# Zeros on TensorE, four-way scores, and copies moved between VectorE and ScalarE in a two-layer vision tower

## The reference

```python
h = _L0_tok_ref(x, W, b)                       # patches @ W.T + b: (64, 64, 64)
h = h + _L0_attn_ref(_layernorm(h), ...)       # attention in 64 windows of 64 tokens, 8 heads of 8
h = h + _L0_ffn_ref(_layernorm(h), ...)        # graph-attention router, top 2 of 4 experts
h = h + _L1_attn_ref(_layernorm(h), ...)       # one head of 64, batch norm, relu
h = h + _L1_ffn_ref(_layernorm(h), ...)        # top 2 of 8 experts

def _L0_attn_ref(x, w_qkv, b_qkv, w_proj, b_proj, rel_pos_bias):
    qkv = (x @ w_qkv + b_qkv).reshape(NWb, W, 3, NUM_HEADS, HEAD_DIM).transpose(2, 0, 3, 1, 4)
    q, k, v = (qkv[0], qkv[1], qkv[2])
    attn = jnp.einsum('nhqd,nhkd->nhqk', q, k) * HEAD_DIM ** (-0.5)
    attn = jax.nn.softmax(attn + bias[None], axis=-1)      # bias[h, q, k] = rel_pos_bias[h, k - q + 63]
    out = jnp.einsum('nhqk,nhkd->nhqd', attn, v).transpose(0, 2, 1, 3).reshape(NWb, W, D)
    return out @ w_proj + b_proj
```

## Time and profile before

| what | value |
|---|---|
| device time of three runs | 793.17, 797.44, 798.47 us; median 797.44 |
| profiled execution | 796.66 us, its span 794.8 us |
| mean granted TensorE clock | 0.744 of full speed |
| busy: TensorE, its weight loads | 538.0 us (68%), 309.7 us (39%) |
| busy: VectorE | 561.4 us (71%) |
| busy: ScalarE, GpSimd | 350.3 us (44%), 279.0 us (35%) |

### The profile page before, as it was taken

The page is one execution under the profiler, slowest core; times in us unless marked ns, Lnnn a source line. Parts: engine busy times, 40 slices in busy tenths (PEclk is TensorE's granted clock), DMA queues, the critical chain, the costliest instruction groups (busy, mean ns, idle before and its releaser), DMA issues. The chain is left out here.

```text
span 794.8 us, 12363 instructions
## 1 busy us (share of the span) xinstructions
PE 538.0 (68%) x4174; PEld 309.7 (39%) x4179; DVE 561.4 (71%) x1303; ACT 350.3 (44%) x833; POOL 279.0 (35%) x340
## 2 busy tenths in 40 slices
PE   5606968499899785366567277724368848788986
PEld 4503535266566462133233234311246524222322
DVE  6994997988987585789997489885523466467453
ACT  1115536247577432244343134387533434555453
POOL 6003111112122023777777578700211102144334
PEclk9998557659899695555565565658569967799898
DMA  6100000000000005111111111000000000000001
GB/s 191 38 0 1 1 1 1 1 1 2 1 2 2 3 0 72 23 39 27 35 38 24 21 23 38 8 2 0 0 1 1 1 0 1 1 0 2 14 13 27
DMA packets 28632, 13.04 MB, mean 16 GB/s; under 512 B 22080, under 2 KB 25761, under 8 KB 28322
## 3 DMA queue, kind: packets, MB, share of 16 engines
q1 hardware_dynamic: 23842, 10.82, 5.5%
q0 software_dynamic: 4736, 1.51, 2.2%
HBM read 10.77 MB, written 1.54 MB: 15 GB/s over the span
## 5 line engine op out<-in xcount | busy, mean ns | idle before, releaser
L1532 POOL DMA_INDIRECT edge_scratch<-src_rows_dram,slot_src_index x144 | 152.9, 1062 | 46.5 <-issue 43.4
L607 POOL TENSOR_TENSOR wa_kbd<-wa_qk,headmask 128x512 f32<-128x512 f32 x32 | 35.3, 1104 | 157.1 <-ACT wa_qk L717 157.1
L494 POOL TENSOR_TENSOR ln_xs<-xn,ln_stats 128x256 f32<-128x256 f32 x32 | 19.7, 622 | 160.6 <-DVE ln_stats L462 94.7
L736 ACT ACTIVATE wa_probs<-wa_scores,wa_max 128x64 f32<-128x64 f32 x256 | 64.4, 335 | 8.1 <-DVE wa_max L784 7.9
L2015 DVE SCALAR_TENSOR_TENSOR moe_weighted<-moe_y_ps,moe_b_cols,moe_G 128x512 f32<-128x512 f32 x32 | 24.0, 750 | 47.1 <-ACT moe_G L1988 44.2
L2074 POOL TENSOR_TENSOR moe_acc<-moe_acc,moe_weighted 128x512 f32<-128x512 f32 x28 | 37.7, 1348 | 49.7 <-DVE moe_weighted L2015 49.6
L1703 PE MATMUL moe_h_ps<-xT,moe_w 65*128 65x512 f32 x64 | 54.3, 996 | 0.0
L1695 PE MATMUL edge_acc<-edge_scratch 128*64 128x64 bf16 x672 | 22.3, 236 | 47.2 <-DVE edge_scratch L118 47.2
L1974 ACT ACTIVATE moe_hidden<-moe_h_ps,moe_b_cols 128x1024 f32<-128x1024 f32 x32 | 35.5, 1113 | 41.1 <-PE moe_h_ps L1906 41.1
L555 PE MATMUL ln_pT<-ident,ln_xs 128*64 128x128 f32 (+1 forms) x112 | 22.1, 341 | 45.3 <-POOL ln_xs L494 44.4
L647 PE MATMUL wa_s_ps<-wa_kbd,wa_qk 64*64 64x512 f32 x128 | 45.7, 799 | 4.3 <-issue 3.7
(11 more groups left out here) (404 smaller groups left out, 1369.1 us busy)
## 6 DMA issues: line engine op xcount, KB each, us to landing
edge_onehot_T<-slot_lo_dram SPq DMA_DIRECT2D x16, 288.0 KB, 3.2
edge_scratch<-src_rows_dram,slot_src_index POOLq DMA_INDIRECT x144, 2.5
edge_scratch<-in_L_ffn_edge_index SPq DMA_DIRECT2D x2, 1024.0 KB, 6.3
xrow<-in_x SPq DMA_DIRECT2D x4, 256.0 KB, 7.7
out_h<-h SPq DMA_DIRECT2D x4, 256.0 KB, 2.6
moe_w<-in_L_ffn_W SPq DMA_DIRECT2D x3, 256.0 KB
src_rows_dram<-src_rows SPq DMA_DIRECT2D x1, 320.0 KB
moe_w<-in_L_ffn_W SPq DMA_DIRECT2D x2, 128.0 KB
```

Of the source, the lines that this page charges most:

```text
L607: pool.tensor_tensor(kbd[b][:], bc_at(qk[b][:, 1, :], 1, NH), bc(k.headmask[:, 0, :], WIN), ALU.mult).then_inc(kbd_ready, 1)
L736: ins = act.activation(pr[b][:, h, :], sc[b][:, h, :], ACT.Exp, bias=mx[b][:, h:h + 1], scale=-1.0)
L1532: pool.indirect_dma_start(gs[b][:, j, :], None, srow_dram, bass.IndirectOffsetOnAxis(edges.src_index[:, x:x + 1], axis=0))\
```

## The change

- **tokenize.** The reordering of the pixels (`take`) and the storing of the tokens (`save`) move from VectorE to ScalarE. VectorE makes the 16 pulls in a row, right after the weights' copy. `pick`, `pick_small`, the selects and the cast go.
- **First normalize.** After its statistics VectorE makes three pulls. PREFIX_STEP and MOVE_STEP become 6 and 11.
- **Scores.** The masked keys hold four heads at a time: row group g of a window (dimensions 32 g to 32 g + 31) holds heads 4 g to 4 g + 3, masked by a new 128x4 mask that VectorE makes at the start. Each tile has four products of 32 rows by 256 columns; group g goes to bank g of one score tile, which is used for every tile (`biased >= c`).
- **Zeros.** Ahead of the wait for the exponentials, TensorE multiplies zeros three times, 128x128 by 512 columns in bf16, into the bank that the turned exponentials then overwrite.
- **Router.** The two casts of the edge parts move to ScalarE; VectorE's second and third step stand between `match`, `spread` and the new `spread_far`.
- **Combine.** The block goes. VectorE weighs and adds quarters 2 and 3 right after the gates, ahead of the adds of quarters 0 and 1.

```diff
-PREFIX_STEP, MOVE_STEP, RING, AHEAD = 7, 12, 6, 2
+PREFIX_STEP, MOVE_STEP, RING, AHEAD = 6, 11, 6, 2
...
         @block.scalar
         def _(act):
-            for c in range(n):
+            def take(c):
+
+                act.wait_ge(loaded[c], 16)
+                if c > 1:
+                    act.wait_ge(turned, c - 1)
+                act.activation(patch[c % 2][:].rearrange("s j (p q) -> s j p q", p=8),
+                               xrow[c][:].rearrange("s (p j q) -> s j p q", p=8, j=8), ACT.Copy).then_inc(cut, 1)
...
+            def save(c):
+
+                act.wait_ge(mapped, c + 1)
+                act.activation(h[:, 8 * c:8 * c + 8, :], ph[c % 2][:], ACT.Copy).then_inc(saved, 1)
+
             take(0)
...
             take(1)
             for c in range(n):
+                turned_out(c)
                 if c + 2 < n:
                     take(c + 2)
                 save(c)
...
+        @block.vector
+        def _(dve):
+            for b in range(2):
+                dve.memset(xT[b][D:D + 1, :], 1.0).then_inc(ones, 1)
+            dve.wait_ge(weight_turned, 1)
+            dve.tensor_copy(k.wtok[0:D, :], weight_ps[:]).then_inc(weight_ready, 1)
+            for _ in range(16):
+                next(lists, None)
...
-            dve.tensor_copy(k.pick[:].rearrange("r p t (x m) -> r (p t x) m", x=2),
-                            bc(k.pick_small[:].rearrange("r p t x -> r (p t x)"), D))
...
+            if beside and not N:
+                for c in range(3):
+                    beside(dve, c)
...
-    kbd = [mem.sb(f"wa_kbd{b}", [P, NH, WIN]) for b in range(2)]
+    kbd = [mem.sb(f"wa_kbd{b}", [P, NH // 2, WIN]) for b in range(2)]
+    mask = mem.sb("wa_headmask", [P, NH // 2])
...
-    s_ps = [mem.ps(f"wa_s_ps{b}", [P, NH, WIN]) for b in range(2)]
+    s_ps = mem.ps("wa_s_ps", [P, 2, 2, NH // 2, WIN])[:, :, 0]
...
             def scores(c, b, first):
                 pe.wait_ge(qk_ready, c + 1)
                 pe.wait_ge(kbd_ready, c + 1)
-                if not first:
-
-                    pe.wait_ge(biased, c - 1)
+                if c:
+
+                    pe.wait_ge(biased, c)
                 pe.sem_inc(k.pe_passed, 1)
-                for r in range(2):
-                    half = slice(r * D, (r + 1) * D)
-                    ins = pe.matmul(s_ps[b][half], qk[b][half, 0, :], kbd[b][half])
+                for g in range(2):
+                    for r in range(2):
+                        dims = slice(r * D + g * D // 2, r * D + (g + 1) * D // 2)
+                        ins = pe.matmul(s_ps[r * WIN:(r + 1) * WIN, g], qk[b][dims, 0, :], kbd[b][dims])
                 ins.then_inc(scores_done, 1)
 
+            zeros = k.zero_mm[:].bitcast(BF16)
+
             def turn(c, b, first):
-                pe.wait_ge(exp_done, c + 1)
                 if not first:
                     pe.wait_ge(probsT_ready, c - 1)
+                for _ in range(3):
+                    pe.matmul(t_ps[b][:], zeros[:, 0:P], zeros[:, 0:512])
+                pe.wait_ge(exp_done, c + 1)
...
                 chunk(c)
                 if c + 2 < RCHUNKS:
                     match(c + 2)
+                second(c)
                 if c + 1 < RCHUNKS:
                     spread(c + 1)
+                third(c)
+                if c + 1 < RCHUNKS:
+                    spread_far(c + 1)
...
             choose(1)
+            for x, q in enumerate((2, 3)):
+                y, part = ys[q], h[:, 8 * q:8 * q + 8, :]
+                after(dve.tensor_tensor(y, y, bc(gates[:, 8 * q:8 * q + 8, :], D), ALU.mult))
+                after(dve.tensor_tensor(y[:, :, 0:2, :], y[:, :, 0:2, :], y[:, :, 2:4, :], ALU.add))
+                after(dve.tensor_tensor(y[:, :, 0, :], y[:, :, 0, :], y[:, :, 1, :], ALU.add))
+                dve.tensor_tensor(part, part, y[:, :, 0, :], ALU.add)
...
                 act.activation(val[c % 2][:, :, :, GE], ee[c % 2][:, 0], ACT.Exp).then_inc(exp_done, 1)
+                act.wait_ge(weighted, c + 1)
+                if c > 1:
+                    act.wait_ge(summed, c - 1)
+                act.activation(parts[c % 2][:, :, 0, :], val[c % 2].rearrange("p c h e -> p c (h e)"), ACT.Copy)\
+                   .then_inc(first_part, 1)
+                act.wait_ge(part_left, c + 1)
+                act.activation(parts[c % 2][:, :, 1, :], left, ACT.Copy).then_inc(second_part, 1)
...
-def combine(nc, mem, k, ys, gates, h):
...
-            norm("ln0")
+            def pull_early(dve, c):
+                next(lists, None)
+
+            norm("ln0", beside=pull_early)
...
-            with stage() as m:
-                combine(nc, m, k, ys, gates[0], h)
```

More of the change, by code:

```diff
@@ L273, in tokenize @@
         mem.sem(f"{x}_loaded") for x in ("wtok", "window_bias", "constants"))
-    filled, padded, xT_padded, selected, masked, picked, ones = (
+    filled, padded, xT_padded, selected, masked, ones = (
         mem.sem(x) for x in ("constants_filled", "weights_padded", "xT_padded", "constants_selected",
-                             "headmask_made", "pick_made", "patch_ones"))
+                             "headmask_made", "patch_ones"))
     weight_turned, weight_ready, bias_turned, folds = (
@@ L385, in _ @@
                                pT[c % 2][:].rearrange("k j s -> k s j"), ACT.Copy).then_inc(copied, 1)
+            def save(c):
+                act.wait_ge(mapped, c + 1)
+                act.activation(h[:, 8 * c:8 * c + 8, :], ph[c % 2][:], ACT.Copy).then_inc(saved, 1)
+            take(0)
+            take(1)
+            for c in range(n):
+                turned_out(c)
+                if c + 2 < n:
+                    take(c + 2)
+                save(c)
             act.wait_ge(bias_turned, 1)
@@ L585, in window_attention @@
              "max_done", "exp_done", "rsum_done", "probs_turned", "probsT_ready",
-             "o_done", "o_scaled", "o_turned", "oT_ready", "proj_done", "added", "zeroed", "ones")
+             "o_done", "o_scaled", "o_turned", "oT_ready", "proj_done", "added", "zeroed", "ones", "mask_ready")
     (qkv_done, qk_ready, kbd_ready, v0_ready, vbd_ready, scores_done, biased, max_done,
      exp_done, rsum_done, probs_turned, probsT_ready, o_done, o_scaled, o_turned, oT_ready,
-     proj_done, added, zeroed, ones) = (mem.sem("wa_" + x) for x in names)
+     proj_done, added, zeroed, ones, mask_ready) = (mem.sem("wa_" + x) for x in names)
     n = TILES
@@ L805, in _ @@
                 dve.memset(vbd[b][:], 0.0).then_inc(zeroed, 1)
+            dve.tensor_tensor(mask[:], k.headmask[:, 0, 0:NH // 2], k.headmask[:, 0, NH // 2:NH],
+                              ALU.add).then_inc(mask_ready, 1)
             dve.wait_ge(zeroed, 2)
@@ L1412, in _ @@
             spread(0)
+            spread_far(0)
             dve.tensor_copy(iota16[:], k.iota_lo[:]).then_inc(iota_ready, 1)
@@ L1825, in choose @@
         yield
-def combine(nc, mem, k, ys, gates, h):
-    first, last = 2, 3
-    weighted, halved, quartered, scaled = (
-        mem.sem("combine_last_" + x) for x in ("weighted", "halved", "quartered", "scaled"))
-    def tiles(q):
-        return slice(8 * q, 8 * q + 8)
-    with nc.Block() as block:
-        @block.vector
-        def _(dve):
-            for x, q in enumerate((first, last)):
-                y = ys[q]
-                if q == first:
-                    dve.tensor_tensor(y, y, bc(gates[:, tiles(q), :], D), ALU.mult).then_inc(weighted, 1)
-                    dve.wait_ge(weighted, 1)
-                else:
-                    dve.wait_ge(scaled, 8 * E0)
-                dve.tensor_tensor(y[:, :, 0:2, :], y[:, :, 0:2, :], y[:, :, 2:4, :], ALU.add).then_inc(halved, 1)
-                dve.wait_ge(halved, x + 1)
-                dve.tensor_tensor(y[:, :, 0, :], y[:, :, 0, :], y[:, :, 1, :], ALU.add).then_inc(quartered, 1)
-                dve.wait_ge(quartered, x + 1)
-                dve.tensor_tensor(h[:, tiles(q), :], h[:, tiles(q), :], y[:, :, 0, :], ALU.add)
-        @block.scalar
-        def _(act):
-            for t in range(8):
-                for e in range(E0):
-                    act.activation(ys[last][:, t, e, :], ys[last][:, t, e, :], ACT.Copy,
-                                   scale=gates[:, 8 * last + t, e:e + 1]).then_inc(scaled, 1)
 def experts(nc, mem, k, x2, logits, gates, h, out):
```

52 lines of the change are left out of this document (15 added, 37 removed).

## The result

The changed kernel took 752.81 us (median of four executions, 750.42 to 758.81) against 795.83 us for the kernel before; the ratio is 0.9471, 95% interval 0.9403 to 0.9539. The prediction said 767 us and 756 to 782, so the direction was right, and the gain of 43 us is 1.4 times the one forecast and outside the range. A second set of executions gave 760.37 us and 0.9564 [0.9496, 0.9631]. Two of its four, 765.36 and 769.55 us, are over 1.5% above its fastest; the other two alone are at 0.949. The eight executions together run from 750.42 to 769.55 us with a median of 754.7, and the mean granted clock of each goes from 0.746 for the longest to 0.779 for one of 753.47: the longest executions are those with the lowest clocks.

What follows compares the result with a forecast made beforehand. No single bound: VectorE in the first stage, VectorE or TensorE by tile in attention, GpSimd's gathers then VectorE in the router. Terms sum to 30.6 us off 796.66, giving 766.1, plus 0.8: 767 us, range 756 to 782.

Steps and rivals of the forecast that it cites:

- Zeros and mask, +7.0: First attention: three zero products per tile raise TensorE's clock (4.6 us) and the shorter mask gives 2.4; sum +7.0.
- One list tile fewer, +2.9: First attention: a 7.16 us list tile goes at the front, one without lists, taken as 4.25, comes at the end.
- the norm's half microsecond: First normalize: three list pulls fit VectorE's idle time to within 0.1 us, the block's closing adds some 0.4: -0.5 us.
- First stage, +8.1: Start to first normalize: copies to ScalarE and the unused table gone let lists start 4.8 us earlier; ends 4.6 to 8.3.
- rival C: Second fill holds the lists (3.4 us less), ScalarE's router handovers cost what the casts save (1.5 less): 772; chance 0.10.
- Scores: First attention: four 32-row products run together, about 1.1 us at 1.2 GHz and 0.65 at 2.4, from 1.97 and 1.08.
- Rival A: First attention's scores: only two row groups run together, so the products gain nothing; 8 us less, 775; chance 0.12.
- Router, +1.5: Router: two casts a chunk leave VectorE, gaining 3.0 and 0.2 us; the last chunk's second deviation waits, -1.7.
- quarters, +8.9: Combine: quarters 2 and 3 on VectorE right after the gates; normalize starts at 552.3 us instead of 561.19.
- Rivals B and D: First attention: B, the clock gives nothing, 775, chance 0.15; D, the zeros run on a slow clock, 835, chance 0.04.
- the offset that the prediction added: Whole kernel before: the median of the runs, 797.44 us, is 0.8 above the profiled execution, so 766.1 became 767.
- The longer wait behind the extra edges: Router: a sign that the forecast is right, the wait behind the extra edges 3 to 4 us longer.

Runs made afterwards that it cites:

- first profile: Profiled execution of the changed kernel, nothing further changed, from its first set of executions: 758.81 us, span 756.9 us.
- second profile: The changed kernel run once more, nothing changed, for a second profiled execution: span 751.5 us.
- the two experiments: The changed kernel with the router's two casts per chunk on VectorE again (0.958), and with the old combine block for quarters 2 and 3 (0.9607).

## Why the prediction was right and wrong

*Zeros and mask, +7.0 forecast: the step that failed by its size.* The twenty tiles took 103.6 us before and 90.5 after, 13.1 us. Two sizes in this term were too small. The prediction counted 6.9 us that the clock could give (4.6 us a tile in three tiles, and 1.7 us in two more) and took two thirds of it, "The trace doesn't tell how soon the clock would rise". In the changed kernel none of these five stands at the lower clock: those that took 5.8, 6.4 and 6.7 us take 4.0, 4.2 and 4.6, and the pair of 5.9 and 5.5 us takes 4.2 and 4.3, together 8.9 us. This is the higher clock and the shorter scores and mask in one; the runs don't part them, and the changed kernel without zeros has 6.1 of the 8.9. The other 4.2 us come from tiles that weren't slow. The prediction gave them 2.4, since it stopped half of the mask's gain at "TensorE's 4.5". As TensorE's own time that figure was nearly right (4.43 against 4.50 us with the same list products), but it did not bind in most tiles: the long tile takes 6.9 us in place of 7.8, behind it TensorE has a lead and VectorE's 4.2 us set the tile, and the three tiles of 5.0 us ahead of it, which VectorE set, take 4.5.

*What the prediction treated as separate terms.* It priced the faster scores as room for the zeros and the zeros as a chance on the clock. That pairing was the right mechanism, and the ratios show it: in the kernel before, the zeros alone give 0.2%, which is not told apart from nothing, and the scores alone give 1.1%; from the full change, taking out the zeros costs 0.7 to 1.6 points and the scores 1.9 to 2.9, by which of the changed kernel's two ratios one takes.

*One list tile fewer, +2.9: measured 3.8* (7.2 at the front for 3.4 at the end). The tile without lists was taken as 4.25; at the higher clock and with the shorter scores it is 3.4. The old schedule put back costs 3.4 us net of the norm's half microsecond, where the two terms of the sum gave 2.4.

*First half of attention, 0 forecast: -4.2 in the first profile.* Two tiles without much list work took 4.9 and 6.7 us, the clock at 0.50 from 108 to 125 us, where before they took 3.4 and 4.0. In the second profile they took 3.0 and 3.8. Of the seven profiles with three zeros and the new scores, three have the slow pair and four don't, with the same code in attention's first half in all but one. This is one part of the 5.4 us between the two profiles; the stages from the fourth norm on are another. Three heavy list tiles there gave 2.1 us that the forecast didn't count either (11.5, 11.7 and 11.1 us became 11.1, 10.6 and 10.6).

*First stage, +8.1: right in the first profile (8.5), and rival C's half in the second (4.9).* The prediction asked whether the operation gets in ahead of the second fill, and said 1.3 to 2 instead of 4.8 if not. It does in two profiles of eight and doesn't in six, so the likelier case was the one that it took for the rival, and that the profile behind this result met the term was luck, a matter of 0.1 us in when the edge index landed.

*Scores: right.* 0.66 us at 2.4 GHz and 1.13 at 1.2, against 0.65 and 1.1. Rival A is out. The Trainium skill's rule on banks (TensorEngine Tiling (Array Packing), "Gotcha 1: PSUM Pressure") doesn't hold in its strict form here: two row groups write one bank, in different partitions, and all four end within 0.66 us.

*Router, +1.5 and quarters, +8.9: right,* 1.5 to 1.7 and 9.0 by the two experiments, 11.0 together in the table.

*Rivals B and D.* The clock did answer, and no tile with zeros took 8 us. Of B's case there was something: zeros alone, in the kernel before, raise the clock and still give nothing.

*What lay outside the sum.* The stretch between the third and the fourth norm, which no edit touches, took 2.3 us less, and from the fourth norm on the two profiles of the changed kernel differ by 4.8 us with the same code. Nothing was run to tell how much of the 2.3 us is the change's doing. By parts, of the 14 us between 767 and 752.8, 7.3 are the sum's (37.9 for 30.6, of which attention has 4.4 and the stretches from the third norm on 2.8), 6.0 are the profiled execution of the changed kernel against its median (758.81 against 752.81), and 0.8 the offset that the prediction added. The range allowed 3 us for the clock in later stages, too little for the second part alone.

*The signs named.* The first list operation near 10.3 us (10.05), the norm at about 45 (45.3), score groups at 0.65 (0.66) and the norm 9 us closer behind the gates (9.0) came; the second of them only in the profiles whose first list operation wasn't held. A clock above 0.85 over attention came only in the second profile (0.87; 0.80 in the first). The longer wait behind the extra edges did not: it is 6.7 us as before, while VectorE's waits for the gathers ahead of it grew from 6.9 to 15.9 us.

## What to carry to other kernels

Price two edits together when one makes idle time on TensorE and the other fills it: here the zeros alone were worth nothing and the scores alone about 1%, and the zeros on top of the scores were worth 0.7 to 1.6 points. Filler products are nearly free up to the time that the next-slowest engine leaves (three cost up to 0.3 us in some tiles here; three more cost 0.5 to 1.0 us in most). Where two engines take turns as the bound, a floor read from one of them holds only once its lead is used up. And cut long fills into pieces where another engine's first operation may start beside them: the operation gained up to 3.4 us, though the whole time didn't tell it apart.

## What the runs showed of the hardware that was not expected

A fill of one partition by 4096 columns holds GpSimd as long as one of 128 partitions (3.51 us both), and it held a VectorE operation that had started 0.05 us ahead of it for 3.4 us, while at 0.17 us ahead the operation kept its 1.23 us and the fill grew by 1.0. Shorter work on TensorE went with a lower clock: with the shorter scores alone the mean granted clock of five executions was 0.719 to 0.739, where 39 executions of the kernel before had 0.731 to 0.759. Identical code differed by 19 us over eight executions in two sets, with clocks from 0.746 to 0.779; four executions don't settle a change of 1% in this kernel.
